# Self attention: rows normalised on ScalarE with scale and offset from GpSimd, and five regrouping DMAs a turn issued by GpSimd

## The reference

```python
B, S, E = 16, 256, 128          # 16 heads of 8
x = x + _L0_attn_ref(_layernorm(x, axis=-1), ...)      # block-local attention, 8 global tokens
x = x + _L0_xattn_ref(_layernorm(x, axis=-1), ctx_768, ...)
x = x + _L0_ffn_ref(_layernorm(x, axis=-1), ...)       # 16 experts, top 2, and a shared expert

def _layernorm(x, axis=-1, eps=1e-05):
    m = jnp.mean(x, axis=axis, keepdims=True)
    v = jnp.var(x, axis=axis, keepdims=True)
    return (x - m) / jnp.sqrt(v + eps)
```

## Time and profile before

| | us |
|---|---|
| median of three runs | 567.36 (565.86 to 570.26) |
| profiled execution, its time | 572.98 |
| its span, first to last instruction | 571.1 |
| TensorE busy in the span | 487.5 |
| VectorE busy | 408.1 |
| ScalarE busy | 297.4 |
| GpSimd busy | 288.6 |
| thirteen turns of self attention, 51.49 to 219.97 | 168.48 |

### The profile page before, as it was taken

The page is one execution under the profiler, slowest core; times in us unless marked ns, Lnnn a source line. Parts: engine busy times, 40 slices in busy tenths (PEclk is TensorE's granted clock), DMA queues, the critical chain, the costliest instruction groups (busy, mean ns, idle before and its releaser), DMA issues. The chain is left out here.

```text
span 571.1 us, 16500 instructions
## 1 busy us (share of the span) xinstructions
PE 487.5 (85%) x5675; PEld 363.8 (64%) x5675; DVE 408.1 (71%) x1245; ACT 297.4 (52%) x757; POOL 288.6 (51%) x540
## 2 busy tenths in 40 slices
PE   1978989899989899878989999999867999999810
PEld 1756666667666666546767777677644888888610
DVE  7567989999888888867987898788472343433337
ACT  2573665555656665425664666465424534444237
POOL 5543434433333343101276788777772477777720
PEclk9997999999999999979997999899988999999985
DMA  6626343545655656216232333322125443343159
GB/s 192 111 53 136 62 63 62 110 107 108 109 108 101 112 103 137 64 47 139 65 80 71 98 85 99 89 73 81 33 67 144 114 113 111 110 115 94 53 173 291
DMA packets 96002, 58.30 MB, mean 102 GB/s; under 512 B 24560, under 2 KB 92224, under 8 KB 95920
## 3 DMA queue, kind: packets, MB, share of 16 engines
q1 hardware_dynamic: 74448, 40.00, 30.3%
q10 hardware_dynamic: 16896, 7.34, 6.5%
q0 software_dynamic: 4576, 9.91, 5.2%
HBM read 20.83 MB, written 17.50 MB: 67 GB/s over the span
## 5 line engine op out<-in xcount | busy, mean ns | idle before, releaser
L507 POOL TENSOR_SCALAR veps<-mv 128x2 f32<-128x2 f32 x48 | 10.8, 225 | 159.3 <-issue 101.4
L1278 ACT ACTIVATE probs<-ps 128x512 f32<-128x512 f32 x128 | 73.2, 602 | 12.1 <-PE ps L1658 10.0
L602 POOL DMA_INDIRECT expert_in<-xn,sloti x64 | 65.6, 1025 | 17.9 <-issue 17.9
L1133 DVE TENSOR_TENSOR eh<-ps,sg 128x256 f32<-128x256 f32 x40 | 17.0, 425 | 59.1 <-ACT sg L1482 58.1
L761 DVE TENSOR_REDUCE nmax<-ps 128x8 f32<-128x512 f32 x64 | 42.5, 686 | 18.9 <-PE ps L1593 18.8
L655 POOL DMA_INDIRECT expert_out<-ey,xt x40 | 38.3, 958 | 27.6 <-DVE ey L1140 17.1
L761 DVE TENSOR_REDUCE mparts<-ps 128x8 bf16<-128x512 f32 x64 | 43.3, 685 | 6.3 <-PE ps L1648 5.9
L1593 PE MATMUL ps<-kbd,qs 96*64 96x128 bf16 x512 | 38.1, 293 | 4.5 <-DMA qs<-part 2.5
L2005 PE MATMUL ps<-wgu,turned 128*128 x160 | 41.2, 380 | 0.0
L1476 ACT COPY turned<-ps 128x512 f32<-128x512 f32 (+1 forms) x43 | 23.8, 554 | 27.7 <-PE ps L1998 23.2
L509 POOL TENSOR_TENSOR rstd<-veps,minus_half 128x2 f32<-128x2 f32 x48 | 35.6, 742 | 4.0
(11 more groups left out here) (247 smaller groups left out, 1387.4 us busy)
## 6 DMA issues: line engine op xcount, KB each, us to landing
kbd<-part SPq DMA_DIRECT2D x192, 32.0 KB
qs<-part ACTq DMA_DIRECT2D x93, 64.0 KB
xt<-expert_in SPq DMA_DIRECT2D x64, 72.0 KB
qs<-part SPq DMA_DIRECT2D x51, 64.0 KB
ck_scr<-wgu SPq DMA_DIRECT2D x6, 512.0 KB
ckbd<-ck_scr SPq DMA_DIRECT2D x16, 192.0 KB
kbd<-part SPq DMA_DIRECT2D x48, 64.0 KB
wgu<-in_L_ffn_gate_up_w SPq DMA_DIRECT2D x4, 512.0 KB, 3.9
```

The lines of the kernel that those rows point to most:

```text
L602: pool.indirect_dma_start(xs, bass.IndirectOffsetOnAxis(sloti[b % 3][:, n:n + 1], 0), xn3[b % 3][:, n // TOPK, n % TOPK, :], None).then_in ...
L1278: a_.activation(probs[:, 2 * i:2 * i + 2, :], P2[i % 2][:, :].rearrange("p (j q) -> p j q", j=2), ACT.Exp, scale=SCALE).then_inc(s("probs" ...
```

## The change

From batch 3 on, VectorE no longer normalises the rows of self attention. GpSimd makes, beside 1/sqrt(variance + eps), the negative mean (`drop`) and their product (`offset`), in `self_scale_and_offset`, four operations for two. ScalarE writes `xn` as x * rstd + offset in two activations (`self_normalised`), for batch b+2 in turn b, between its cast of the second part and its copy to `xnT`. The cross attention's rows stay on VectorE.

From batch 2 on, five of the 18 regrouping DMAs are issued by GpSimd (`later_parts_regrouped`): the two query DMAs of part 1, and of part 2 the query DMA and the two key DMAs. They count up a semaphore of their own, `lent`. SyncE keeps ten key DMAs, ScalarE three query DMAs. Whoever waited for `got` now waits for `got` and `lent`.

```diff
@@ sync @@
-                        if K_PART[i] == k:
+                        if K_PART[i] == k and (b < FIRST_LENT or k < 2):
...
-                wait_apart(sp, (s_("got"), GOT[True] * b + GOT[True]))
+                wait_apart(sp, (s_("got"), self_got(b + 1)), (s_("lent"), self_lent(b + 1)))
@@ gpsimd @@
+            def self_scale_and_offset(b):
+
+                wait_apart(pool, (s_("aggr"), 2 * b + 2), (s_("norm"), 2 * b))
+                g.tensor_scalar(veps[:, :], mv[:, :, 1], EPS, None, ALU.add).then_inc(s_("veps"), 1)
+                g.tensor_scalar(drop[:, :], mv[:, :, 0], -1.0, None, ALU.mult).then_inc(s_("veps"), 1)
+                pool.wait_ge(s_("veps"), self_rooted(b) + 2)
+                g.tensor_tensor(rstd[:, :], veps[:, :], minus_half[:, :], ALU.pow).then_inc(s_("veps"), 1)
+                pool.wait_ge(s_("veps"), self_rooted(b) + 3)
+                g.tensor_tensor(offset[:, :], drop[:, :], rstd[:, :], ALU.mult).then_inc(s_("rstd"), 1)
...
+            def later_parts_regrouped(b, p):
+
+                at_least(pool, s_("pair"), 4 * (b - 1))
+                for k in (1, 2):
+                    pool.wait_ge(s_("part"), 3 * b + k + 1)
+                    for i in range(NP):
+                        if Q_PART[i] == k:
+                            pool.dma_start(qs[p][16 * i:16 * i + 16, :, :], part[:, k, 0:S]).then_inc(s_("lent"), 16)
+                        if K_PART[i] == k == 2:
+                            for a in range(2):
+                                pool.dma_start(kbd[p][16 * i + 8 * a:16 * i + 8 * a + 8, :, a, :, :].rearrange("r j k n -> r j (k n)"),
+                                               part[64 * a:64 * a + 64, k, S:2 * S]).then_inc(s_("lent"), 16)
...
                     self_global_heads(b + 1, 1 - p)
+                    if b + 1 >= FIRST_LENT:
+                        later_parts_regrouped(b + 1, 1 - p)
...
-                    rstd_of(s_, b + 3)
+                    self_scale_and_offset(b + 3)
@@ vector @@
-                if has(b + 3):
-                    normalise(s_, b + 3)
-                elif CROSS and b + 3 < B + 3:
+                if CROSS and B <= b + 3 < B + 3:
@@ scalar @@
+            def self_normalised(b):
+
+                act.wait_ge(s_("rstd"), b + 1)
+                act.wait_ge(s_("xT_ps"), b)
+                for u in range(2):
+                    a_.activation(xn[:, u, :], X[:, 2 * b + u, :], ACT.Identity, bias=offset[:, u:u + 1], scale=rstd[:, u:u + 1]).then_inc(s_("norm"), 1)
...
-                at_least(act, s_("got"), GOT[True] * b)
+                at_least(act, s_("got"), self_got(b))
+                at_least(act, s_("lent"), self_lent(b))
...
-                if b != 1:
+                if b == 0:
                     queries_regrouped(b, p, 1)
...
-                    if b > 0:
-                        queries_regrouped(b + 1, 1 - p, 2)
...
                 if has(b + 2):
+                    if b + 2 >= SCALED:
+                        self_normalised(b + 2)
                     self_columns(b + 2)
@@ tensor @@
-                    pe.wait_ge(s_("got"), GOT[True] * b + GOT[True])
+                    pe.wait_ge(s_("got"), self_got(b + 1))
+                    at_least(pe, s_("lent"), self_lent(b + 1))
```

More of the change, by code:

```diff
@@ L159, in decoder @@
         rstd = sb("rstd", [128, 2])
+        drop, offset = sb("drop", [128, 2]), sb("offset", [128, 2])
         xn = sb("xn", [128, 2, E])
@@ L335, in decoder, with self_rooted @@
         CROSS = "B" in phases
+        SCALED = 3
+        def self_rooted(b):
+            return b + 2 * max(b - SCALED, 0)
         def routed(b):
@@ L349, in decoder, with self_got, self_lent @@
         PLANNED = 14
-        GOT = {True: 16 * 3 * NP, False: 16 * NP}
+        GOT = 16 * NP
+        FIRST_LENT, LENT = 2, 5
+        def self_got(n):
+            return 16 * (3 * NP * n - LENT * max(n - FIRST_LENT, 0))
+        def self_lent(n):
+            return 16 * LENT * max(n - FIRST_LENT, 0)
         def sent_back(q):
@@ L432, in regroup_cross @@
                              ck_scr[:, :, :, 2 * M * b:2 * M * (b + 1)].rearrange("i r j n -> (i r) j n")).then_inc(w_("ck_put"), 16)
-                sp.wait_ge(c_("got"), GOT[False] * (b + 1))
+                sp.wait_ge(c_("got"), GOT * (b + 1))
             sp.wait_ge(w_("laid_out"), 2)
@@ L690, in stats @@
                 for u in range(2):
-                    wait_apart(dve, (s("stats"), 2 * b + u + 1), (s("veps"), b))
+                    wait_apart(dve, (s("stats"), 2 * b + u + 1), (s("veps"), self_rooted(b) if s is s_ else b))
                     v.bn_aggr(mv[:, u, :], st[:, u, :]).then_inc(s("aggr"), 1)
@@ L1290, in cross_first_part @@
                 if b == 0:
-                    act.wait_ge(s_("got"), GOT[True] * B)
-                at_least(act, c_("got"), GOT[False] * (b - 1))
+                    act.wait_ge(s_("got"), self_got(B))
+                    act.wait_ge(s_("lent"), self_lent(B))
+                at_least(act, c_("got"), GOT * (b - 1))
                 at_least(act, c_("part"), 3 * b)
@@ L1639, in cross_scores @@
                     pe.wait_ge(w_("ck_put"), 16 * (NP + b + 1))
-                    pe.wait_ge(c_("got"), GOT[False] * (b + 1))
+                    pe.wait_ge(c_("got"), GOT * (b + 1))
                     if b == 0:
```

## The result

The changed kernel takes **575.09 us** (median of 6 runs, 572.16 to 579.50) where the kernel before takes 566.84 (6 runs, 565.86 to 570.26). The ratio is 1.011, with a 95% interval of 1.007 to 1.015 (the two medians alone stand at 1.0146, its upper end): slower by about one per cent. The forecast of 565.0 with no difference is wrong; 575.09 is close to the time of the second rival (late landing, 574.7), which had been given 0.08. That the two numbers agree so closely is luck, as the part on the prediction shows.

What follows compares the result with a forecast made beforehand. The bound was a loop over VectorE, then ScalarE and TensorE. Waits and late issues (1.78) plus the context turn (0.6) gave -2.4 us, set against the median of 567.36: 565.0, range 561 to 580.

Steps and rivals of the forecast that it cites:

- the second rival: Queries lent to GpSimd land late (1.49 a turn) without GpSimd being full: +9.7 - 2.4, 574.7 us; chance 0.08.
- The loop runs over VectorE and then ScalarE and TensorE, and L699 is in neither half: Self-attention turn: removing VectorE's normalisation, up to 1.00 us each, is worth nothing in an undisturbed turn of 12.73.
- The gain forecast for the turn with two context pieces: In the turn from 103.04, where VectorE is the late one, dropping its normalisation gains 0.6 us.
- ScalarE's two activations, 0.77 to 1.02, are covered: On ScalarE from 75.25, they end before TensorE needs the rows at 76.49, leaving 0.2 to 0.5; counted as nothing.
- GpSimd's issue, 1.26 from the indirect DMAs of the earlier trace: Each of GpSimd's five lent DMA issues takes 1.26 us; the fifth ends at 81.55, just before the scale is due.
- Rival 1: GpSimd becomes the bound through its five issues ahead of the scale: 597 us at 2.0 an issue, 571 at 1.6; chance 0.16.
- The landing: Lent queries land 2.23 us after their issue starts, at 82.82, 0.63 ahead of the scores due at 83.45; no wait left.
- upper bound of 3.39: Slower landing row, from SyncE's late turn: 3.39 us from end of issue to landing, putting the queries at 84.94, 1.49 late.
- The DMA waits and late issues go, 1.78.: Over the thirteen self-attention turns, the excess above undisturbed time outside the turn from 103.04 goes: 2.99 - 1.21 = 1.78 us.
- A landing late by w costs w/2 a turn: Scores waiting for regrouped pieces: lateness in every turn costs about half, since it gives the following turn slack.
- The copies lose nothing beside descriptor writing: VectorE's copies on the loop (L772) stay at the median 0.42 us beside GpSimd's DMA issues.
- Rival 3: VectorE's two copies a turn wait for GpSimd's descriptor writing: 590 us at 0.96 each, 571 at 0.23; chance 0.06.

Runs made afterwards that it cites:

- norm_only: The changed kernel without the lending: ScalarE normalises, but every transfer is issued where the kernel before issues it; 567.75 us, ratio 1.001 to the kernel before.
- lend_keys: The kernel before, but GpSimd issues only the third part's two key pieces, with its memset ahead of them; 569.03 us, ratio 0.996 to the kernel before.
- lend_queries_memset: The changed kernel, but SyncE issues all twelve key pieces, GpSimd three query pieces with its memset ahead; 569.64 us, ratio 1.001 to the kernel before.
- lend_only: The changed kernel with the normalise back on VectorE; GpSimd still issues the five lent pieces; 575.19 us, ratio 1.015 to the kernel before.

## Why the prediction was wrong, step by step

**The loop runs over VectorE and then ScalarE and TensorE, and L699 is in neither half.** Right: undisturbed turns stay at 12.74 with VectorE 1.00 less busy, and norm_only is at 1.001. The gain forecast for the turn with two context pieces came too: 13.29 (from 105.77) where the earlier trace rows has 13.94.

**ScalarE's two activations, 0.77 to 1.02, are covered.** Right: 0.87 for the two together (0.484 each, overlapping), and norm_only shows no cost.

**GpSimd's issue, 1.26 from the indirect DMAs of the earlier trace rows.** Wrong in size: 0.54 to 0.58. Rival 1, GpSimd as the bound, rested on this and is out: GpSimd, its DMA issues counted, is busy 7.46 of 12.74. Taken alone, this error made the forecast too cautious.

**The landing, "GpSimd's last output DMA ended 2.23 after the start of its issue ... I take GpSimd's own row, so no wait is left".** This is the step that failed. The row was the last of the experts' outputs, with no other transfer beside it. In the loop the lent pieces take 3.7 to 4.1 in the median and up to 6.1; the five have landed at 11.08 behind the cast in the median, 5.0 behind the end of the last issue (6.05), past even the upper bound of 3.39. What was saved on the issue (2.95 us in the turn above) and more was lost in flight. And the sum asked only when the lent pieces land. It had no term for what they do to the others: SyncE's ten end their issue at 6.85 and land at 11.55, a flight of 4.7 where the kernel before has 2.7 (8.19 to 10.88), and they are the last in every turn.

**"The DMA waits and late issues go, 1.78."** Wrong too, and for the same reason: the excess of the waits for the key tile went from 1.6 to 4.7 us. The prediction took SyncE's last two issues for the ones that ended the waits of the earlier trace rows. The eleven kernels with ten issues on SyncE land between 10.39 and 11.55 (the kernel before, with twelve, at 10.88); the one that took other traffic away lands at 9.88 with all twelve. What flies beside the keys moves the landing more than the number of SyncE's issues, and in none of the eleven did taking issues to another queue gain anything clear of the noise.

**A landing late by w costs w/2 a turn.** Roughly borne out: the scores start 0.67 later in the mean, 13 x 0.67 / 2 = 4.4, and the thirteen turns took 4.74 more. Two things that are no landing are in both numbers: the stretch at the low clock (its scores come 12.78 behind the cast, though all pieces had landed at 9.60) and the long copy. Of the 4.74, 3.1 are waits for the key tile.

**The copies lose nothing beside descriptor writing.** Right in the median (0.422) and for the DMA issues nearly so, but the prediction did not follow what the five issues push: GpSimd's memset, moved onto a copy. The longer copies come to 0.5 us in the changed kernel and 1.95 us where three pieces are lent. Rival 3 had the mechanism and the wrong partner.

Rival 2 was the nearest: the landing is late without a full GpSimd. But it had the lent pieces land last, and SyncE's do, and its price, 9.7, was twice what the turns show, since the lateness was 0.67 in the mean and not 1.49. That its 574.7 lies beside the measured 575.09 is luck: the rest of the 8 us between the medians lies outside the thirteen turns or in differences of a size that the runs of one kernel also show among themselves, and was not assigned to a cause.

One candidate is TensorE's clock. The mean granted clock is 0.949 over the six runs of the changed kernel and 0.956 over the 114 runs of the kernel before that stand beside the experiments, and a lower clock goes with a longer time in the kernel before too (564.76 at 0.963, 573.06 at 0.948). In the changed kernel's trace TensorE had waited 1.50 for the key tile, until 85.71, before the clock fell at 88.20; the wait of 1.58 until 166.06 is followed by no such fall. Whether the late landing lowers the clock was not tested.

Also open is why two or three lent pieces are harmless and five are not. The traces show how far each goes: from 5 to 8 us behind the cast SyncE's queue moves 150 KB in small packets in the kernel before, 105 with two or three lent pieces (lend_keys, lend_queries_memset) and 71 with five. The Trainium skill (DMA: Bandwidth & Descriptors, section "Queues, rings and completion order") says that each engine takes turns between queues packet by packet. If the packets that the trace counts are these, mean packets of 1.6 KB in GpSimd's queue against the 512 bytes of the key pieces' would favour the lent pieces over the keys. The slowed queue of SyncE fits, but no run changed the size of a packet alone.

## What to carry to other kernels

Moving an issue to another engine saved issue time only; if the same bytes still fly beside the rest, the landing need not come earlier, and here, with five pieces through GpSimd, it came later, for the pieces of the other queue too. Price a landing from a row with the same traffic beside it, never from a lone transfer at the end of a stage. And when instructions are put into an engine's row, look at each instruction that they push back and at what it will now run beside.

## What the runs showed that was not expected

VectorE's subtraction `res` (L747 before, L789 after) went from a mean of 0.681 to 0.762 although nothing of it was changed, and to 0.770 in norm_only, while it stays at 0.681 in lend_only. It starts as far behind the first part's cast as before, but GpSimd's mask on the global probabilities (L581 before, L623 after) now comes later and runs into it: GpSimd's two more operations for scale and offset have pushed the mask back (in norm_only it runs from the offset to the mask without idle time there, where before it waited 0.77 ahead of `xg`). In norm_only and then in the kernel before:

```profile
58.16 0.61 POOL L623 TENSOR_TENSOR probs_g<-probs_g,constants 128x256 f32<-128x256 f32 x1
58.27 1.05 DVE L789 TENSOR_TENSOR res<-qk,part 128x512 f32<-128x512 f32 x1
...
58.73 1.20 POOL L571 TENSOR_TENSOR kg<-qk,constants 128x16 f32<-128x16 f32 x3
```
```profile
59.75 0.62 POOL L581 TENSOR_TENSOR probs_g<-probs_g,constants 128x256 f32<-128x256 f32 x1
...
60.25 0.68 DVE L747 TENSOR_TENSOR res<-qk,part 128x512 f32<-128x512 f32 x1
60.32 1.23 POOL L544 TENSOR_TENSOR kg<-qk,constants 128x16 f32<-128x16 f32 x3
```

The subtraction ends 0.55 to 0.57 behind the end of the mask in both, so the 1.05 holds a wait for it. This is not covered: ScalarE's second cast waits for `res`, and the turn with the 1.05 takes 13.10 where an undisturbed one takes 12.74. It happens in five of the thirteen turns of norm_only (four of the changed kernel), 13 x 0.08 = 1.1 us in all, so part of what the change spares VectorE is lost again.
